# Spare bf16 matmuls ahead of the tensor engine's waits in the first and the last part of a four-layer network

## The reference

```
x = layernorm(x + attention(x))                 # 16 heads of 64, softmax, output projection
x = layernorm(x + routed_ffn(x))                # below
x = layernorm(x + attention2(x))                # linear attention and a window of 65 keys, gated together
x = layernorm(x + ffn2(x))                      # causal attention with 16 heads, then a mixture of 8 experts
```

```
cluster = argmax(calibrate(x @ cluster_sigs.T))       # 8 clusters
tile    = argmax(calibrate(x @ sigs.T) in cluster)    # 8 tiles of that cluster
comp    = tanh(gelu(x @ w1 + b1) @ w2 + b2)           # 2 numbers for each token
y       = x + f(comp, tables[tile]) * directions[tile]
```

## Time and profile before

| | |
|---|---|
| time, median of 3 runs | 2400.33 us (2399.95 to 2401.05) |
| the profiled execution's own time | 2394.53 us |
| its span, first to last instruction | 2392.8 us |
| busy share of PE, PEld, DVE, ACT, POOL | 92%, 64%, 65%, 56%, 35% |
| mean granted clock of PE | 0.970 |
| share of the chain that ended last: PE, DVE, ACT, POOL | 77%, 12%, 5%, 4% |

### The profile page before, as it was taken

How to read it: one execution, slowest core, us unless ns; L and a number is a source line. 1 busy time by engine, 2 the same in 40 slices (tenths; PEclk the granted TensorE clock), 3 DMA queues, 4 the chain that set the end, 5 groups by cost and what they waited for, 6 DMA issues and landing times.

```text
span 2392.8 us, 44064 instructions
## 1 busy us (share of the span) xinstructions
PE 2207.2 (92%) x16144; PEld 1537.0 (64%) x16144; DVE 1557.9 (65%) x4247; ACT 1348.8 (56%) x3784; POOL 848.4 (35%) x1010
## 2 busy tenths in 40 slices
PE   8659999999999999999999999999999999998897
PEld 5446666756668566676667666676666856667465
DVE  5567676676657766577755868558676676656642
ACT  5336564764647655476545657366564764546442
POOL 3214561054510643116521346114551064510630
PEclk9879999999999999999999999999999999999899
DMA  4000001000010000110001100100001000010001
GB/s 148 27 1 2 1 2 45 10 32 1 1 53 4 29 1 1 54 33 1 1 10 45 32 1 1 36 19 32 1 1 45 10 32 1 1 45 2 31 1 49
DMA packets 24721, 50.44 MB, mean 21 GB/s; under 512 B 3316, under 2 KB 3900, under 8 KB 24252
## 3 DMA queue, kind: packets, MB, share of 16 engines
q1 hardware_dynamic: 24508, 47.63, 6.2%
HBM read 45.52 MB, written 2.10 MB: 20 GB/s over the span
## 4 chain that ended last, share of the span: by engine, by line
PE 77%; DVE 12%; ACT 5%; POOL 4%; issue 2%; DMA 0%; SPq 0%; DVEq 0%; ACTq 0%
PE ps L1472 10%; PE ps L1493 10%; PE ps L651 5%; PE ps L668 5%; PE ps L602 4%; PE ps L850 4%; PE ps L1410 4%; PE ps L888 4%; PE ps L1505 4%; PE ps L1427 4%; PE ps L781 3%; PE ps L764 3%; PE ps L1365 3%; PE ps L817 2%; PE ps L1376 2%; POOL rn L1715 2%
## 5 line engine op out<-in xcount | busy, mean ns | idle before, releaser
L1030 POOL TENSOR_TENSOR rstd<-ve,half_neg 128x4 f32<-128x4 f32 (+1 forms) x56 | 66.9, 1195 | 979.5 <-DVE ve L1011 979.5
L1493 PEld LDWEIGHTS ps<-wbuf,QK 128*128 128x128 f32 x2048 | 266.0, 191 | 108.2 <-issue 99.9
L1286 POOL TENSOR_TENSOR E<-E,ri 128x512 f32<-128x512 f32 x240 | 247.8, 1041 | 179.7 <-DVE ri L1085 179.1
L1596 ACT ACTIVATE QK<-ps,cols 128x512 f32<-128x512 f32 x256 | 172.9, 687 | 210.1 <-PE ps L1472 209.8
L1472 PE MATMUL ps<-h2T,wbuf 128*128 128x512 f32 x512 | 276.9, 630 | 0.2
L1722 POOL TENSOR_TENSOR work<-work,ri 128x128 f32<-128x128 f32 x480 | 231.8, 508 | 120.8 <-DVE ri L1645 120.0
L1493 PE MATMUL ps<-wbuf,QK 128*128 128x128 f32 x2048 | 270.2, 275 | 0.0
L911 ACT ACTIVATE E<-ps,nm 128x256 f32<-128x256 f32 x480 | 225.5, 484 | 64.3 <-DVE nm L1078 64.0
L1556 ACT ACTIVATE work<-ps,nm 128x128 f32<-128x128 f32 x480 | 198.5, 425 | 99.4 <-DVE nm L1636 99.4
L1715 POOL TENSOR_TENSOR rn<-ss,half_neg 128x8 f32<-128x8 f32 x120 | 195.3, 1638 | 160.1 <-DVE ss L1621 159.3
L1078 DVE TENSOR_REDUCE nm<-ps 128x2 f32<-128x512 f32 x256 | 168.8, 684 | 23.4 <-PE ps L651 21.7
(11 more groups left out here) (280 smaller groups left out, 4490.8 us busy)
## 6 DMA issues: line engine op xcount, KB each, us to landing
wbuf<-in_w SPq DMA_DIRECT2D x128, 256.0 KB, 3.2
xT<-in_xT SPq DMA_DIRECT2D x8, 256.0 KB, 3.5
xr<-in_xr SPq DMA_DIRECT2D x8, 256.0 KB, 4.2
bias_t<-in_bias_t SPq DMA_DIRECT2D x1, 2048.0 KB
out_y<-xn SPq DMA_DIRECT2D x8, 256.0 KB, 2.1
wqkv<-in_wqkv SPq DMA_DIRECT2D x1, 1536.0 KB
wo<-in_wo SPq DMA_DIRECT2D x2, 512.0 KB, 8.2
rows<-in_rows SPq DMA_DIRECT2D x1, 531.0 KB, 7.1
```

The lines of the kernel that those rows point to most:

```text
L1286: nc.gpsimd.tensor_tensor(L.E[:, g % 4, :, :], L.E[:, g % 4, :, :], L.ri[:, g, :].unsqueeze(2).broadcast_to((P, NT, S)), ALU.mult)\
L1493: last = nc.tensor.matmul(bank2[2 + x % 2][:, t * P:(t + 1) * P], hid[:, x % 2, c, t * P:(t + 1) * P], w2[:, x % WB, c, :], start=(c == 0) ...
```

## The change

`spare_work` is called at ten more places, under `if not both`, that is in the first and the last part only, and the call of six becomes one of eighteen there. Each call stands directly ahead of a wait of PE. Nothing else is changed: no other engine's program, no order string, no wait. The middle parts keep their six.

```diff
@@ first_pe
+            if not both:
+                spare_work(pe, bank2[3], 13)
             pe.wait_ge(s["x1_ready"], upto("x1_ready", 1))
             transposed(bank1[2], x1).then_inc(s["x1tr"], 1)
             yield
+            if not both:
+                spare_work(pe, bank2[3], 3)
             pe.wait_ge(s["x1T_ready"], upto("x1T_ready", 1))
...
+                spare_work(pe, bank2[3], 3)
             pe.wait_ge(s["gelu_ready"], upto("gelu_ready", 1))
...
+                spare_work(pe, bank2[3], 60)
             pe.wait_ge(s["hot_ready"], upto("hot_ready", 1))
...
+                spare_work(pe, bank2[3], 3)
             pe.wait_ge(s["hotT_ready"], upto("hotT_ready", 1))
...
+                spare_work(pe, bank2[3], 54)
             pe.wait_ge(s["xn_ready"], upto("xn_ready", 1))
             transposed(bank1[2], xn).then_inc(s["xn_tr"], 1)
+                spare_work(pe, bank2[3], 3)
             pe.wait_ge(s["hT_ready"], upto("hT_ready", 1))
...
+                spare_work(pe, bank2[3], 3)
             pe.wait_ge(s["vlin_ready"], upto("vlin_ready", 1))
...
+                spare_work(pe, bank2[3], 22)
             pe.wait_ge(s["klin_ready"], upto("klin_ready", 1))
             pe.wait_ge(s["qlin_ready"], upto("qlin_ready", 1))
@@ second_pe
+                spare_work(pe, bank2[0], 24)
             pe.wait_ge(s["x3_ready"], upto("x3_ready"))
...
-            spare_work(pe, bank2[1], 6)
+            spare_work(pe, bank2[1], 6 if both else 18)
             yield
             pe.wait_ge(s["o2_ready"], upto("o2_ready", 1))
             transposed(bank2[2], xn2).then_inc(s["o2_tr"], 1)
+                spare_work(pe, bank2[1], 3)
             pe.wait_ge(s["o2T_ready"], upto("o2T_ready", 1))
```

## The result

| | before | after |
|---|---|---|
| median of 7 runs | 2399.99 us (2397.6 to 2401.05) | 2382.34 us (2379.26 to 2393.77) |
| ratio | | 0.9938, interval 0.9924 to 0.9952 |
| profiled execution, its span | 2394.53, 2392.8 us | 2379.3, 2377.5 us |
| mean granted clock | 0.970 | 0.986 |

The ratio of 0.9938 is 14.9 us, the medians differ by 17.7, and the two spans by 15.3. The forecast was 13.1 us. The executions of the changed kernel lie 14.5 us apart, those of before 3.5 here and 10.2 in a later set of 15; most of this study turned out to be about that spread. It goes with the clock: the two shortest executions of the changed kernel had a mean granted clock of 0.986, those of 2391.27 and 2393.77 us 0.979 and 0.977.

What follows compares the result with a forecast made beforehand. PE bounds the kernel (busy 92%, 77% of the chain), at half clock in waits at both ends. 8.3 + 6.3 - 1.5 = 13.1 us off 2400.33 gives 2387.2 us; range 2382 to 2394 for 8 in 10.

Steps and rivals of the forecast that it cites:

- What the clock gives back, first part: First part: PE groups from L882 to L749 run at full instead of half clock, 8.3 us gained.
- The spares' price: Spare matmuls at both ends: each 0.22 us at full clock, 0.43 at half; none late at full clock.
- Last part: Last part: L882, L1365, L1459, L1472 and the transposes behind run at full clock, 6.3 us gained.
- (c): Last part, 2254 to 2264, at half clock: if the shift removes it, some 3 us more; nothing counted.
- (a): First part, 2 us idle behind the 60 and the 54: clock may fall once or twice; 1.0 us off.
- (b): Middle parts: low clock stretches change by an unknown amount when work shifts; 0.5 us off, 2 us either way.
- the forecast's case: Whole kernel: the clock holds nearly everywhere, gain 11 to 15 us, 2385.5 to 2389.5 us; chance 0.55.
- the third rival: The clock holds and the low stretch at 2254 goes too: gain 15 to 19 us, 2381.5 to 2385.5; chance 0.09.
- A sign that did not hold: First middle part's routing should start 8 us earlier than 366.06, and the last part's L1383 no less.
- the partial one: Clock falls again in uncovered rests, or a middle-part low stretch grows: gain 5 to 11 us, 2389.5 to 2395; chance 0.27.
- the spares do not keep the clock: Both ends: bf16 identity work might count less than float32 groups; 2398 to 2402 us, no change; chance 0.05.
- run at half and overrun: Mainly the 60 ahead of L711: spares at half clock end late, together 32 us, 2433 us; chance 0.04.

Runs made afterwards that it cites:

- e4: Changed kernel with as many spares at every place but 8 columns instead of 512, the 18 replaced by the original six wide ones; 2400.59 us, ratio 0.9997.
- e2: Changed kernel without the nine new calls of the first part, so spares added in the last part only; 2390.72 us, ratio 0.9955.
- e7: The changed kernel run again without any edit; 2384.95 us, ratio 0.9936.
- e6: Kernel before the change, with only 11 spares added in each middle part; 2396.96 us, ratio 0.9981.
- e3: Changed kernel without the 13 and all calls of three, keeping the long calls (60, 54, 22, 24, 18); 2384.75 us, ratio 0.9938.
- e5: Changed kernel plus 11 spares in each middle part, ahead of three waits; 2382.98 us, ratio 0.9933.

## Why the prediction was right, step by step

- **What the clock gives back, first part**: 8.3 forecast, 8.30 measured at L814, with the single groups as written (L725 1.57, L719 0.63, L900 0.66). e4, with the same calls and no clock given back, shows that calls of spares without their array time give nothing.
- **The spares' price**: 0.22 at full clock, measured 13.12 us for 60, less a drain; 0.43 at half, measured 0.42; nothing late in after's trace. All rests came out as forecast (1.49, 2.11, 2.24, 0.92, 0.85, 0.39 us).
- **Last part**: 6.3 forecast, 8.5 measured. L882 and L1365 gave 3.4 (3.65 forecast; L1383 took 3.70, not 3.43) and L1459 to L1478 gave 2.95 (2.6 forecast). The rest is (c).
- **(c), the stretch at 2254**: "I count nothing" was the step that failed, by 2.1 us. It was put down to the shift alone; e2 shows that the last part's own spares can do it. It is not certain either: e7 has them and the half clock, e6 has neither.
- **(a), the rests of 2 us**: right in kind and size. One fall cost 1.1 to 1.5 us, in four of six traces, which is 0.9 us in the mean, against 1.0 taken off. In after's trace there was none.
- **(b), the middle parts**: 0.5 taken off, with 2 either way; in the two traces they took 1.6 us back, since before's first middle part was a short one (285.7 us, with 3.4 us at half) and after's was 287.0. But over executions their part is larger than the 2 us: e7's six periods take 4.3 us more than after's and 5.9 more than before's.
- **The agreement of the sum is partly luck.** Between the two traces the gain is 15.3 us against 13.1: (a) did not occur (1.0 more), (b) was 1.1 larger than taken off, and (c) added 2.1. The first two cancel. And the median, 2382.34, lies only 0.3 us inside the range, below the forecast's case (2385.5 to 2389.5) and within that of the third rival (2381.5 to 2385.5, chance 0.09), whose mark, the stretch at 2254 at full clock, after's trace has. The gain by the ratio, 14.9 us, lies at the border of the two.
- **A sign that did not hold**: L1383 was to come no less than 8 us earlier than L1365 did. The routing of the first middle part did come 8.4 us earlier (357.70 against 366.06), but L1383 only 7.2 (2210.06 against 2217.30), because of what the middle parts took back.
- **The forecast's case**, that the clock holds nearly everywhere, describes after's trace; the partial one (5 to 11 us, chance 0.27) describes the executions at 2391 to 2394. Both happened, to the same kernel. What was missed is that these were not rivals but shares of the executions.
- **The rivals on the other side** (the spares do not keep the clock, or run at half and overrun) are excluded by e3: under a call that started at half clock it rose after 4.76 us, and none of e3's executions was over 2391.48 us, where these two rivals expected 2398 or more.

What stays open: why a middle part falls into the 289.9 us form, and whether the change makes that more frequent; e4 shows that it comes without it. After's trace and e7's differ by 3.4 us at the first middle part's gate, and one has it twice while the other has none. That the moment at which the low stretch arrives decides is my guess; it was not varied on its own.

## What to carry to other kernels

Spare work ahead of a wait paid here where PE's own groups are links of a chain with nothing beside them: price it by one existing call in the trace, and size it to end just ahead of the data. Closing long rests to about half a us is worth trying, since behind rests of 2 us the clock fell in four traces of six; that it makes the kernel faster was not shown. Look at the clock, not at PE's busy share, for where it is needed. And where a kernel's executions differ by more than the gain, take several traces and compare the lengths of its repeated parts before explaining a median by one trace.

## What the runs showed of the hardware that was not expected

- PE at 24.00 us busy of 24.00 and at half clock (e5): a full queue of small matmuls did not raise the clock again, and cost 10.2 us in a stretch of 35.4. In after's trace PE is busy 9.35 of the 10.00 us from 2189.4 and at half as well, and each of the fourteen traces has 10.2 us at half there, at the end of the last middle part; no run tried spares there.
- The time of a repeated part goes with how much half clock lies in it. Without the middle spares it is 285.6 to 285.7 us with 3.4 us at half, 286.4 to 287.0 with 6.8, and 289.9 with 13.7; with them it is 285.2 to 285.3 with none, but 285.7 or 286.8 to 286.9 with 3.4, so that where the half clock lies matters too. In after's trace the length settles: the six periods from one gate's matmul to the next run 287.02, 286.95, 286.84, 286.79, 286.72 and 286.75. A gain of 8.4 us ahead of them arrived as 6.7 behind them, against a trace of before that began with a short one of 285.7.
